# x of the batches 1 to 7 rounded by a casting transfer, its remainders by an accumulating transfer

## The chip, the cores and the metric

The kernel runs on one core of a Trainium2 chip. The metric is the device time of one execution in microseconds (us); the lower, the better. The kernel before takes 455.5 us in the median of three runs (455.4 to 455.71).

## The reference

The input x has 8 batches of 256 tokens with 1024 features, in float32. Two layers follow one another.

```python
x = x + ffn0(quantize(x))          # quantize: 8 levels of thresholds, each with its step and zero point
x = x + ffn1(cond1(x))
# ffn0: router logits x @ router_w.T over 4 experts, softmax over the best 2, low-rank deltas A (16 x 1024), B
# cond1: x @ W.T + 0.5 * (x @ lora_A[label of the batch]) @ lora_B_w.T
# ffn1: x @ kernel + bias + two low-rank products (one gated for each batch, one shared)
```

Everything that is linear in x is folded into one matrix P of 1024 x 1024, so that the output of a batch is x @ P plus a bias and low-rank terms. The low-rank terms of the first layer depend on the quantised x.

## The kernel before, in words

P is made first, in 16 steps (8 row tiles for each of 2 halves of the columns), each on TensorE from W and the kernel matrix. Each operand of these products is held as a rounded part (`hi`, of a type to which the value is rounded) and the remainder (`lo`), and a product is three matmuls: hi x hi, hi x lo, lo x hi.

Then comes the loop over 8 batches with 8 slots each, 64 slots q in all. The output of a batch has 4 tiles (2 blocks of tokens, 2 halves of the columns), and two slots make one tile: a matmul of the bias (L1088) opens it, then 12 matmuls a slot (4 of the 8 feature tiles k, three products each: L1090 x_hi by p_hi, L1091 x_hi by p_lo, L1092 x_lo by p_hi), and `close` (L1067) adds the low-rank terms from zt and tb. zt of a batch holds three things: u-projections of x, made by `z_begin` from xs, the unrounded x (L994, L998, in slot 4 of the batch before); the turned gated middle (`gated_turn` L980, copied by ACT in L493); and, when `z_end` (L1005) has closed the former, ACT's copy of it (L635). Only after that copy may TensorE run the `close` of the batch.

The quantisation of batches runs ahead of the products, in 64 groups (8 batches x 8 levels), laid over the slots by the table `GROUPS`. A group is, on ACT, `levels` (L426) and `raise_levels` (L439), on DVE a TENSOR_SCALAR (L662), the mask (L671, a TENSOR_SCALAR) and the merge (L680, COPY_PREDICATED). The first group of a batch also has ACT's magnitude (L416). `mid` (L970) on TensorE then projects the quantised batch. The engines' programs are written out by hand: each runs its own list in its own order and waits on semaphores.

The places that the change touches:
- POOL's queue holds only `quant_input`: the loads of x into xq, for the quantisation, of the batches 1 to 7 (L303). The load for batch c waits until all the levels of batch c - 2 are made.
- SP's queue loads x into xs (L383 for batch 0, `xs_load` L385 to L390 for the others), the adapters and rows, and stores the output (L399, L404).
- `x_part` on ACT (L495 to L502) rounds xs into x_hi, in two parts of 128 x 1024 elements for a batch; `x_part` on DVE (L789 to L793) subtracts x_hi from xs into x_lo. For batch 0 both come right before the loop; for batch b + 1 they come in batch b, on ACT in the slots 1 and 3 (`XAT` in L238, called at L648), on DVE one slot later (L874).
- x_hi and x_lo have two places each, used in turn; `x_done` says that a batch's matmuls have read theirs (L1094).
- TensorE waits for x_lo at the first slot of each batch (L1074).
- Ahead of the loop, after the last P step, DVE also makes the bias (L864), ACT bu (L509).

Of the kernel before, what the change touches and what calls it, by code (L numbers as in the profile page):

```python
# [26 lines left out]
F32 = mybir.dt.float32  # L27
# [4 lines left out]
ALU = mybir.AluOpType  # L32
ACT = mybir.ActivationFunctionType
# [3 lines left out]
BATCH = 8  # L37
# [15 lines left out]
STEPS = HALVES * KT  # L53
# [10 lines left out]
def build(nc, a, out_t, itok):  # L64
# [98 lines left out]
    sem = nc.alloc_semaphore  # L163
# [34 lines left out]
    mg_made, mgt_full, mgt_made = sem("mg_made"), sem("mgt_full"), sem("mgt_made")  # L198
    x_hi_made, x_lo_made = sem("x_hi_made"), sem("x_lo_made")
    bet_hi_made, bet_lo_made, bpfull, bp_made = sem("bet_hi_made"), sem("bet_lo_made"), sem("bpfull"), sem("bp_made")  # L200
# [36 lines left out]

    XAT, ZAT = (1, 3), 4  # L238

# [52 lines left out]
    with nc.allow_non_contiguous_dma(reason="rows of 1 KB and small constants"), nc.Block() as block:  # L292

        @block.gpsimd
        def _(pool):

            def quant_input(c):
                if c == 1:
                    pool.wait_ge(w_in[0], 16 * 2)
                if c >= 2:  # L300
                    pool.wait_ge(levels_made, (c - 1) * G)
                    pool.wait_ge(abs_made, c - 1)
                pool.dma_start(xq[:, c % 2], x_v[c]).then_inc(xq_in[c % 2], 16)  # L303

            for c in range(1, BATCH):
                quant_input(c)

        @block.sync
        def _(sp):
# [75 lines left out]
            def xs_load(b):  # L385
                sp.wait_ge(x_lo_made, b * XPARTS)
                sp.wait_ge(z_read, b)
                sp.dma_start(xs, x_v[b]).then_inc(xs_in, 16)
                if b + 1 < BATCH:
                    adapters(b + 1)  # L390
# [21 lines left out]
        def _(act):  # L412
# [81 lines left out]

            def x_part(c, p):  # L495
                act.wait_ge(xs_in, 16 * (c + 1))
                if c < 2:
                    act.wait_ge(ofull, STEPS)
                else:
                    act.wait_ge(x_done, c - 1)  # L500
                part = slice(p * XK, (p + 1) * XK)
                nc.scalar.activation(x_hi[:, c % 2, part], xs[:, part], ACT.Copy).then_inc(x_hi_made, 1)  # L502

# [118 lines left out]
            for p in range(XPARTS):  # L622
                x_part(0, p)
            for c, g in GROUPS[STEPS + 1]:
# [3 lines left out]
            for q in range(BATCH * KT + LAG + 1):  # L628
# [19 lines left out]
                if b + 1 < BATCH and j in XAT:  # L648
                    x_part(b + 1, XAT.index(j))
                if b + 1 < BATCH and j == ZAT:  # L650
# [6 lines left out]
        def _(dve):  # L657
# [130 lines left out]

            def x_part(c, p):  # L789
                dve.wait_ge(x_hi_made, c * XPARTS + p + 1)  # L790
                part = slice(p * XK, (p + 1) * XK)
                nc.vector.tensor_tensor(x_lo[:, c % 2, part], xs[:, part], x_hi[:, c % 2, part].bitcast(F32),
                                        ALU.subtract).then_inc(x_lo_made, 1)  # L793
# [67 lines left out]
            for p in range(XPARTS):  # L861
                x_part(0, p)
            dve.wait_ge(bias_hi_made, 1)
            nc.vector.tensor_tensor(bias[R:2 * R], bias_raw[R:2 * R], bias[R:2 * R].bitcast(F32),  # L864
                                    ALU.subtract).then_inc(bias_made, 1)
            for b in range(BATCH):
                for j in range(KT):
                    ranks(slot(b, j))
                    for c, g in GROUPS[slot(b, j)]:
                        quant(c, g)  # L870
                    if b == 0 and j == 0:
                        for h in range(HALVES):
                            bp_add(h)
                    if b + 1 < BATCH and j - 1 in XAT:  # L874
                        x_part(b + 1, XAT.index(j - 1))

        @block.tensor
        def _(pe):
# [191 lines left out]
            for q in range(BATCH * KT):  # L1070
                b, j = divmod(q, KT)
                n, part = divmod(q, 2)
                s, (t, h) = b % 2, divmod(n % TILES, HALVES)
                if j == 0:  # L1074
                    pe.wait_ge(x_lo_made, (b + 1) * XPARTS)
                if part == 0:
# [77 lines left out]
```

## Time and profile before

| | us |
|---|---|
| median of 3 runs | 455.5 |
| the profiled execution's own time | 455.03 |
| its span, first to last instruction | 453.2 |
| TensorE (PE) busy | 445.7, 98% |
| DVE busy | 392.8, 87% |
| ACT busy | 357.7, 79% |
| POOL busy | 7.9, 2% |
| DMA from POOL's queue (q0) | 7.34 MB, 4.8% of the 16 engines' span |
| DMA from SP's queue (q1) | 42.66 MB, 29.6% |

PE is TensorE's matmul, PEld its weight load; DVE is VectorE, ACT ScalarE, POOL GpSimd, SP SyncE. Busy times of PE are modelled from pipelined matmuls, so a busy PE does not mean PE at its peak. L502 is line 502 of the kernel. A wait is the idle time of an engine ahead of an instruction, with what released it. The granted clock of TensorE is at full speed over the whole run (1.000).

### The profile page before, as it was taken

To read this page: it belongs to the slowest core of one execution; us is meant where nothing else is said; L and a number is where in the kernel's file an instruction comes from. 1 tells how busy PE (TensorE), PEld (TensorE's weight loads), DVE (VectorE), ACT (ScalarE), POOL (GpSimd) and SP (SyncE) were. 2 spreads that over 40 slices of the span, in tenths; PEclk is the share of its full clock that TensorE was granted. 3 is DMA by queue.
4 is the path that set the end of the run, shared out by engine and by line. 5 is a ranking of instruction groups with operands and counts; after the bars stand their busy time and mean duration, and the time that the engine had idled before them with its cause. 6 is when DMAs were issued, how large, how long until landed. Compare 5 with 4: busy or idle time off the path is not lost.

```text
span 453.2 us, 5629 instructions
## 1 busy us (share of the span) xinstructions
PE 445.7 (98%) x2166; PEld 348.3 (77%) x2166; DVE 392.8 (87%) x392; ACT 357.7 (79%) x296; POOL 7.9 (2%) x11
## 2 busy tenths in 40 slices
PE   8979999999999999999999999999999999999997
PEld 8847778888878887778767877777778777867883
DVE  1696979999999999999999999999987999899410
ACT  1579999946989969898997899959697899778002
POOL 0000000000000000100000000000200000000000
PEclk9999999999999999999999999999999999999999
DMA  7999535200562153214125107105414003101102
GB/s 271 358 311 410 140 82 175 58 1 0 167 204 92 53 135 100 78 39 156 59 93 162 59 25 232 58 2 162 152 31 132 29 29 140 58 1 46 48 1 93
DMA packets 36124, 50.35 MB, mean 111 GB/s; under 512 B 26658, under 2 KB 26914, under 8 KB 33826
## 3 DMA queue, kind: packets, MB, share of 16 engines
q1 hardware_dynamic: 35090, 42.66, 29.6%
q0 software_dynamic: 1008, 7.34, 4.8%
q8 instruction: 17, 0.28, 0.3%
q14 instruction: 9, 0.07, 0.1%
HBM read 39.51 MB, written 10.49 MB: 110 GB/s over the span
## 4 chain that ended last, share of the span: by engine, by line
PE 92%; SPq 4%; DMA 3%; issue 1%; ACT 0%
PE bank L1090 13%; PE bank L1092 13%; PE bank L1091 13%; PE bank L970 6%; PE bank L1067 6%; PE bank L1027 6%; PE bank L1032 6%; PE bank L1028 6%; PE bank L998 6%; PE bank L939 5%; DMA lb<-lb_in 3%; PE bank L1088 2%; PE bank L994 2%; PE bank L1005 1%; PE bank L958 1%; SPq L327 1%
## 5 line engine op out<-in xcount | busy, mean ns | idle before, releaser
L680 DVE COPY_PREDICATED val<-inside,val 128x2048 f32<-128x2048 uint8 x56 | 143.3, 2559 | 0.3
L439 ACT ACTIVATE val<-level,shift,small 128x2048 f32<-128x2048 int16 x64 | 133.9, 2093 | 3.7 <-PE bank L970 3.7
L426 ACT ACTIVATE level<-xq,inv 128x2048 int16<-128x2048 f32 x64 | 127.7, 1997 | 0.6
L1090 PE MATMUL bank<-p_hi,x_hi 128*128 128x512 f32 x256 | 102.8, 402 | 0.0
L1092 PE MATMUL bank<-p_hi,x_lo 128*128 128x512 f32 x256 | 100.1, 391 | 0.0
L1091 PE MATMUL bank<-p_lo,x_hi 128*128 128x512 f32 x256 | 100.0, 391 | 0.0
L662 DVE TENSOR_SCALAR val<-val,width,unshift 128x2048 f32<-128x2048 f32 x64 | 87.2, 1363 | 3.1 <-ACT val L439 3.0
L671 DVE TENSOR_SCALAR inside<-absx,thr 128x2048 uint8<-128x2048 f32 x56 | 72.7, 1299 | 0.0
L1090 PEld LDWEIGHTS bank<-p_hi,x_hi 128*128 128x128 f32 x256 | 48.1, 188 | 17.1 <-issue 8.5
L1091 PEld LDWEIGHTS bank<-p_lo,x_hi 128*128 128x128 f32 x256 | 48.1, 188 | 10.5 <-issue 0.7
L1092 PEld LDWEIGHTS bank<-p_hi,x_lo 128*128 128x128 f32 x256 | 48.1, 188 | 10.5
L1027 PE MATMUL bank<-kp_hi,w_hi 128*128 128x512 f32 x128 | 51.1, 399 | 2.1 <-DVE kp_lo L728 2.1
L1032 PE MATMUL bank<-kp_hi,w_lo 128*128 128x512 f32 x128 | 50.4, 394 | 0.0
L1028 PE MATMUL bank<-kp_lo,w_hi 128*128 128x512 f32 x128 | 49.9, 390 | 0.0
L1067 PE MATMUL bank<-tb,zt 128*128 128x512 f32 x64 | 32.1, 595 | 0.0
L970 PEld LDWEIGHTS bank<-ra,val 128*128 128x128 f32 x256 | 29.8, 192 | 1.8 <-issue 1.4
L1027 PEld LDWEIGHTS bank<-kp_hi,w_hi 128*128 128x128 f32 x128 | 24.1, 188 | 7.1 <-issue 2.5
L970 PE MATMUL bank<-ra,val 128*128 128x68 f32 x256 | 29.5, 273 | 0.0
L998 PE MATMUL bank<-xs,ub 128*64 128x256 f32 x128 | 29.3, 382 | 0.0
L939 PE MATMUL bank<-aefft,wst 128*128 128x256 f32 x128 | 29.2, 380 | 0.0
L1032 PEld LDWEIGHTS bank<-kp_hi,w_lo 128*128 128x128 f32 x128 | 24.1, 188 | 5.3
L1028 PEld LDWEIGHTS bank<-kp_lo,w_hi 128*128 128x128 f32 x128 | 24.1, 188 | 4.7
(98 smaller groups left out, 447.0 us busy)
## 6 DMA issues: line engine op xcount, KB each, us to landing
xs<-xt_in SPq DMA_DIRECT2D x8, 1024.0 KB, 4.9
wst<-w_in SPq DMA_DIRECT2D x14, 512.0 KB, 5.0
xq<-xt_in POOLq DMA_DIRECT2D x7, 1024.0 KB, 6.6
out_t<-ost SPq DMA_DIRECT2D x14, 512.0 KB, 4.0
la<-la_in SPq DMA_DIRECT2D x4, 512.0 KB, 5.4
kst<-k_in SPq DMA_DIRECT2D x4, 512.0 KB, 13.7
lb<-lb_in SPq DMA_DIRECT2D x4, 512.0 KB, 14.4
kst<-k_in SPq DMA_DIRECT2D x1, 2048.0 KB, 10.8
```

Of the source, the lines that this page charges most:

```text
L426: nc.scalar.activation(level[:, g % 2], xq[:, c % 2], ACT.Copy, scale=inv[:, group(g)]).then_inc(levels_made, 1)
L439: nc.scalar.activation(val[:, turn(c, g)], level[:, g % 2], ACT.Relu, bias=shift[:, group(g)], scale=par[:, 1, group(g)]).then_inc(raised, 1)
L662: nc.vector.tensor_scalar(v, v, width[:, group(g)], unshift[:, group(g)], ALU.min, ALU.add).then_inc(valued, 1)
L671: nc.vector.tensor_scalar(inside[:, g % 2], absx, thr[:, group(g)], None, ALU.is_gt).then_inc(masked, 1)
L680: nc.vector.copy_predicated(val[:, acc(c)], inside[:, g % 2], val[:, turn(c, g)]).then_inc(merged, 1)
L970: last = mm(midbank[:, t * RT:(t + 1) * RT], val[:, acc(c), k, t * P:(t + 1) * P], ra[:, k], start=k == 0, stop=k == KT - 1)
L1027: mm(obank[n % RING], w_hi[side(n)][:, o], kp_hi[:, o], start=o == 0, stop=False)
L1028: mm(obank[n % RING], w_hi[side(n)][:, o], kp_lo[:, o], start=False, stop=False)
L1032: last = mm(obank[n % RING], w_lo[side(n)][:, o], kp_hi[:, o], start=False, stop=o == KT - 1)
L1090: mm(o, x_hi[:, s, k, at], p_hi[:, h, k], start=False, stop=False)
L1091: mm(o, x_hi[:, s, k, at], p_lo[:, h, k], start=False, stop=False)
L1092: last = mm(o, x_lo[:, s, k, at], p_hi[:, h, k], start=False, stop=False)
```

## The change

Batch 0 stays as it was. For the batches 1 to 7, POOL issues a transfer of x from memory into x_hi that casts to the rounded type. ACT writes the negative of x_hi into x_lo, in two parts, now in the slots 2 and 4 of the batch before. POOL issues for each part a transfer of x that adds to what stands in x_lo, so that x_lo becomes x minus x_hi. DVE's subtraction goes for these batches. POOL's queue has a new order: the loads of xq for the batches 1 to 3, then for each batch c its `x_split` and after it the load of xq for batch c + 3. TensorE waits at the start of a batch for x_hi and for both additions, and the load of xs by SP waits only for batch 0's x_lo and for the reading of xs by TensorE.

```diff
--- before.py
+++ after.py
@@ -196,7 +196,8 @@
     mid_made, gate_step, gap_made, exp_made = sem("mid_made"), sem("gate_step"), sem("gap_made"), sem("exp_made")
     gates_made = sem("gates_made")
     mg_made, mgt_full, mgt_made = sem("mg_made"), sem("mgt_full"), sem("mgt_made")
-    x_hi_made, x_lo_made = sem("x_hi_made"), sem("x_lo_made")
+    x_hi_made, x_lo_made, x_hi_in, x_neg_made, x_lo_in = (
+        sem(n) for n in ("x_hi_made", "x_lo_made", "x_hi_in", "x_neg_made", "x_lo_in"))
     bet_hi_made, bet_lo_made, bpfull, bp_made = sem("bet_hi_made"), sem("bet_lo_made"), sem("bpfull"), sem("bp_made")
     bp_lo_made, bp_copied = sem("bp_lo_made"), sem("bp_copied")
     mg_zeroed = sem("mg_zeroed")
@@ -235,7 +236,7 @@
     OUT_AT = OUT
     OUT = {at: c for c, at in OUT_AT.items()}
 
-    XAT, ZAT = (1, 3), 4
+    XAT, ZAT = (2, 4), 4
 
 
     V_AT = (4, 10)
@@ -302,8 +303,23 @@
                     pool.wait_ge(abs_made, c - 1)
                 pool.dma_start(xq[:, c % 2], x_v[c]).then_inc(xq_in[c % 2], 16)
 
+            def x_split(c):
+                if c == 1:
+                    pool.wait_ge(ofull, STEPS)
+                else:
+                    pool.wait_ge(x_done, c - 1)
+                pool.dma_start(x_hi[:, c % 2], x_v[c]).then_inc(x_hi_in, 16)
+                for p in range(XPARTS):
+                    part = slice(p * XK, (p + 1) * XK)
+                    pool.wait_ge(x_neg_made, (c - 1) * XPARTS + p + 1)
+                    pool.dma_start(x_lo[:, c % 2, part], x_v[c][:, part], accum_op=ALU.add).then_inc(x_lo_in, 16)
+
+            for c in range(1, 4):
+                quant_input(c)
             for c in range(1, BATCH):
-                quant_input(c)
+                x_split(c)
+                if c + 3 < BATCH:
+                    quant_input(c + 3)
 
         @block.sync
         def _(sp):
@@ -383,7 +399,7 @@
             sp.dma_start(xs, x_v[0]).then_inc(xs_in, 16)
 
             def xs_load(b):
-                sp.wait_ge(x_lo_made, b * XPARTS)
+                sp.wait_ge(x_lo_made, XPARTS)
                 sp.wait_ge(z_read, b)
                 sp.dma_start(xs, x_v[b]).then_inc(xs_in, 16)
                 if b + 1 < BATCH:
@@ -492,14 +508,17 @@
                     act.wait_ge(ofull, STEPS + (c - ZSLOTS + 1) * TILES)
                 nc.scalar.activation(zt[2 * R:P, c % ZSLOTS], mgbank[ER:2 * ER, 0:TOK], ACT.Copy).then_inc(mgt_made, 1)
 
-            def x_part(c, p):
-                act.wait_ge(xs_in, 16 * (c + 1))
-                if c < 2:
-                    act.wait_ge(ofull, STEPS)
-                else:
-                    act.wait_ge(x_done, c - 1)
+            def x_part(p):
+                act.wait_ge(xs_in, 16)
+                act.wait_ge(ofull, STEPS)
                 part = slice(p * XK, (p + 1) * XK)
-                nc.scalar.activation(x_hi[:, c % 2, part], xs[:, part], ACT.Copy).then_inc(x_hi_made, 1)
+                nc.scalar.activation(x_hi[:, 0, part], xs[:, part], ACT.Copy).then_inc(x_hi_made, 1)
+
+            def x_neg(c, p):
+
+                act.wait_ge(x_hi_in, 16 * c)
+                part = slice(p * XK, (p + 1) * XK)
+                nc.scalar.activation(x_lo[:, c % 2, part], x_hi[:, c % 2, part].bitcast(F32), ACT.Copy, scale=-1.0).then_inc(x_neg_made, 1)
 
             def bu_out(c):
 
@@ -620,7 +639,7 @@
             p_out(STEPS - 1)
 
             for p in range(XPARTS):
-                x_part(0, p)
+                x_part(p)
             for c, g in GROUPS[STEPS + 1]:
                 quant(c, g)
             bp_lo_out()
@@ -646,7 +665,7 @@
                 if slot(b, j) in EXP:
                     gate_exp(EXP[slot(b, j)])
                 if b + 1 < BATCH and j in XAT:
-                    x_part(b + 1, XAT.index(j))
+                    x_neg(b + 1, XAT.index(j))
                 if b + 1 < BATCH and j == ZAT:
                     bu_out(b + 1)
             for n in range(BATCH * TILES):
@@ -786,10 +805,10 @@
                 nc.vector.tensor_tensor(mg[:, :, ER:2 * ER].rearrange("p t (e r) -> p t e r", e=E), mid[:, :, 0:ER].rearrange("p t (e r) -> p t e r", e=E),
                                         gates.unsqueeze(3).to_broadcast([P, TT, E, R0]), ALU.mult).then_inc(mg_made, 1)
 
-            def x_part(c, p):
-                dve.wait_ge(x_hi_made, c * XPARTS + p + 1)
+            def x_part(p):
+                dve.wait_ge(x_hi_made, p + 1)
                 part = slice(p * XK, (p + 1) * XK)
-                nc.vector.tensor_tensor(x_lo[:, c % 2, part], xs[:, part], x_hi[:, c % 2, part].bitcast(F32),
+                nc.vector.tensor_tensor(x_lo[:, 0, part], xs[:, part], x_hi[:, 0, part].bitcast(F32),
                                         ALU.subtract).then_inc(x_lo_made, 1)
 
             for m in range(KT // 4, KT // 2):
@@ -859,7 +878,7 @@
                 ranks(n)
             p_out(STEPS - 1)
             for p in range(XPARTS):
-                x_part(0, p)
+                x_part(p)
             dve.wait_ge(bias_hi_made, 1)
             nc.vector.tensor_tensor(bias[R:2 * R], bias_raw[R:2 * R], bias[R:2 * R].bitcast(F32),
                                     ALU.subtract).then_inc(bias_made, 1)
@@ -871,8 +890,6 @@
                     if b == 0 and j == 0:
                         for h in range(HALVES):
                             bp_add(h)
-                    if b + 1 < BATCH and j - 1 in XAT:
-                        x_part(b + 1, XAT.index(j - 1))
 
         @block.tensor
         def _(pe):
@@ -1071,8 +1088,11 @@
                 b, j = divmod(q, KT)
                 n, part = divmod(q, 2)
                 s, (t, h) = b % 2, divmod(n % TILES, HALVES)
-                if j == 0:
-                    pe.wait_ge(x_lo_made, (b + 1) * XPARTS)
+                if q == 0:
+                    pe.wait_ge(x_lo_made, XPARTS)
+                elif j == 0:
+                    pe.wait_ge(x_hi_in, 16 * b)
+                    pe.wait_ge(x_lo_in, 16 * b * XPARTS)
                 if part == 0:
                     if n < RING:
                         pe.wait_ge(ofree, STEPS)
```

## Rows read from the trace of the kernel before

**Rows 1.** busy time of TensorE, and the chain that ended last (page)
```profile
PE 445.7 (98%) x2166; PEld 348.3 (77%) x2166; DVE 392.8 (87%) x392; ACT 357.7 (79%) x296; POOL 7.9 (2%) x11
...
PE 92%; SPq 4%; DMA 3%; issue 1%; ACT 0%
```

**Rows 2.** TensorE's waits: for what, us in total, times, longest
```profile
PE bank L1027 <- DVE kp_lo L728: 2.1, 1, 2.1
```

**Rows 3.** groups of lines: busy us, mean ns | idle before
```profile
L792 DVE TENSOR_TENSOR x_lo<-xs,x_hi 128x1024 fp32r<-128x1024 f32 x16 | 19.9, 1249 | 0.7 <-ACT x_hi L502 0.7
...
L502 ACT ACTIVATE x_hi<-xs 128x1024 fp32r<-128x1024 f32 x16 | 16.7, 1047 | 0.4 <-DMA xs<-xt_in 0.3
```

**Rows 4.** landing of the loads of L303: all seven, then the one at 317.8
```profile
DMA to landing us min/median/max: 5.1/6.6/9.1
...
DMA to landing us min/median/max: 8.0/8.0/8.0
```

**Rows 5.** stretches: busy time of each engine, clock, DMA share, GB/s
```profile
192.00:193.00 1.00, 1.00 (x6) 0.80 (x5) 1.00 (x2) 1.00 (x1) 0.00 (x0) 1.00 1.00 426
...
166.00:167.00 1.00, 1.00 (x6) 0.81 (x6) 1.00 (x2) 0.00 (x0) 0.00 (x0) 1.00 1.01 131
...
320.00:327.00 7.00, 7.00 (x33) 5.30 (x32) 7.00 (x5) 3.02 (x5) 0.17 (x1) 1.00 0.79 246
```

**Rows 6.** ACT's timeline: start us, us, line, operation, idle before
```profile
199.91 0.22 ACT L509 ACTIVATE bu<-bank 64x64 f32<-64x64 f32 x1
...
287.85 0.58 ACT L532 ACTIVATE ost<-bank 128x512 f32<-128x512 f32 x1
...
315.48 2.01 ACT L426 ACTIVATE level<-xq,inv 128x2048 int16<-128x2048 f32 x1
...
321.72 0.38 ACT L493 ACTIVATE zt<-bank 64x256 f32<-64x256 f32 x1 [0.81 <-PE bank L980]
325.27 0.38 ACT L635 ACTIVATE zt<-bank 64x256 f32<-64x256 f32 x1 [3.16 <-PE bank L1005]
```

**Rows 7.** TensorE's timeline
```profile
213.12 0.48 PE L1088 MATMUL bank<-bias,ones 128*128 128x512 f32 x1
...
278.88 1.02 PE L1067 MATMUL bank<-tb,zt 128*128 128x512 f32 x2
...
314.97 0.80 PE L1088 MATMUL bank<-bias,ones 128*128 128x512 f32 x1
...
328.04 1.88 PE L1067 MATMUL bank<-tb,zt 128*128 128x512 f32 x4
...
343.86 3.68 PE L970 MATMUL bank<-ra,val 128*128 128x68 f32 x32
```

**Rows 8.** POOL's timeline
```profile
229.12 0.53 POOL L303 DMA_DIRECT2D xq<-xt_in  x1 [39.54 <-ACT level L426]
...
317.78 2.39 POOL L303 DMA_DIRECT2D xq<-xt_in  x1 [43.83 <-ACT level L426]
```

**Rows 9.** DVE's timeline, end of P and around 318 us
```profile
164.75 1.27 DVE L671 TENSOR_SCALAR inside<-absx,thr 128x2048 uint8<-128x2048 f32 x1
...
317.51 1.34 DVE L662 TENSOR_SCALAR val<-val,width,unshift 128x2048 f32<-128x2048 f32 x1
...
319.96 2.54 DVE L680 COPY_PREDICATED val<-inside,val 128x2048 f32<-128x2048 uint8 x1
```

**Rows 10.** timelines of ACT, DVE and TensorE at the loop's start
```profile
169.92 2.01 ACT L502 ACTIVATE x_hi<-xs 128x1024 fp32r<-128x1024 f32 x2 [0.30 <-DMA xs<-xt_in]
...
181.08 0.37 ACT L493 ACTIVATE zt<-bank 64x256 f32<-64x256 f32 x1
...
173.40 1.22 DVE L864 TENSOR_TENSOR bias<-bias_raw,bias 32x1024 fp32r<-32x1024 f32 x1
...
176.63 0.50 PE L1088 MATMUL bank<-bias,ones 128*128 128x512 f32 x1
...
183.00 0.64 PE L1005 MATMUL bank<-zt,bu 64*64 64x256 f32 x2
```

## The prediction, made before the changed kernel ran

> **What bounds the kernel now.** I read the page first. TensorE is busy for 445.7 of 453.2 us and the chain that ended last is 92% TensorE [rows 1]. Busy matmul time is modelled, so the next view is the list of TensorE's waits: four entries in the whole run, the longest 2.1 us on DVE's kp_lo [rows 2], and asked of 170 to 453 us alone the list is empty. So in the batch loop TensorE waits for nothing, and relief of another engine has nothing there to give back. The change can only make new waits. The working therefore asks, for every edit, at what time its result is wanted and at what time it will be there.
>
> **The change, part by part.** *DVE:* 14 of the 16 subtractions at L792 go, 1249 ns each, 17.5 us [rows 3]. No TensorE wait of the loop ends at DVE, so they are worth nothing; their cover is TensorE's own work. *ACT:* 14 copies at L502 become 14 negations of the same shape, 1047 ns each [rows 3]; I price them the same. They move one or two slots later (slots 2 and 4 of a batch, where they stood in 1 and 3). They now wait for the casting transfer (x_hi), and behind a waiting negation stand, on ACT, the quantisation of the next groups, the evictions (L532) and the zt copy (L635) that TensorE's closing matmuls (L1067) need. *SP:* its loads of xs no longer wait for x_lo, so they come no later than before: nothing. *POOL:* its queue gets 7 casting and 14 accumulating transfers between the loads of xq.
>
> *Casting and accumulating transfers.* The trace has neither. The nearest row is a plain 1 MB load from POOL, 5.1, 6.6 and 9.1 us from issue to landing (minimum, median, maximum) [rows 4]; in the middle it moves 426 GB/s [rows 5], 2.5 us for 1.05 MB. I bound a cast by that below and by twice the movement above (an estimate: 5 us of movement), and take it near the plain one, because size and rows are the same. An accumulation of 512 KB reads two sides, so I bound it by half a plain load below and by 9.1 us above.
>
> *Are the accumulations in time?* The tightest is batch 1. Its second negation stands in slot 4, after the quantisation and ahead of the L509 that ran at 199.91; it ends at about 201.0 [rows 6]. Batch 1 begins with the L1088 at 213.12 [rows 7]. That is 12.1 us for issue and landing, against at most 9.1. In the later batches more work of TensorE lies between slot 4 and the next start, and the same count gives more. Cost: 0.
>
> *Is x_hi in time for the first negation?* It is issued when the batch before last is done and wanted in slot 2 of the next. Tightest where nothing else interferes is batch 4: issue 278.9 at the close of batch 2, ACT free after L635 and L532 at about 287.4 (287.85 + 0.58 less the 1.04 of the L502 that has left) [rows 6, 7]. That is 8.5 us against a median of 6.6: at most a short wait of ACT, and what TensorE wants of ACT next, zt and the eviction, stands ahead of the negation in slot 2. Cost: 0.
>
> *Batch 5 is another matter.* The new order on POOL is xq(7), then x_hi(5), and xq(7) still waits for the last level of batch 5. That level is the L426 which began at 315.48; POOL's L303 followed at 317.78 [rows 6, 8]. TensorE freed the slot for x_hi(5) with batch 3, just ahead of the L1088 at 314.97 [rows 7], so the order costs 3 us at once. And the issue of xq(7) itself held POOL for 2.39 us, where that of 229.12 took 0.53 [rows 8]. In those 2.39 us DVE ran two TENSOR_SCALARs, the first from 317.51, and POOL was free just after COPY_PREDICATED began at 319.96 [rows 9]. The Trainium skill, SBUF — State Buffer, section on who interferes with whom, says that DVE in a mode with both ports locks GpSimd out of the shared pair, so that it cannot write descriptors; the trace agrees (2.39 against 0.53 us). DVE and ACT have the same work between 307 and 318 us as before, so I let the 2.39 us stand; without that lock all of the following comes 1.9 us earlier.
>
> So xq(7) lands at 317.78 + 8.0 = 325.8 [rows 4]. x_hi(5) is behind it in the same queue, with the store of the output beside both. Another 1.05 MB takes 2.5 us at 426 GB/s and 4.3 us at the mean of 320 to 327 us, 246 GB/s [rows 5]; I take 2.9, nearer the former because the queue is full by then. Landing: 328.7. ACT is free for the negation at 322.1, after L493 (321.72 + 0.38) [rows 6], and waits 6.6 us. Then negation 1.05, zt copy 0.38, about 0.1 for handing over: zt stands at 330.2. TensorE wants it for the L1067 at 328.04, whose weights are loaded some 0.2 us earlier [rows 7]. Before, zt was there at 325.65, 2.2 us early. **New wait: 330.2 - 327.8 = 2.4 us**, bounds 2.0 and 3.8 with the two rates, 0.5 without the lock. Behind it ACT is some 5 us late. Its last value for batch 5 (L439) then ends near 334 and DVE's merge some 4 us later, 338; the L970 that wants it begins at 343.86 [rows 7]. The second negation of batch 5 ends near 341, and batch 5 begins a whole L970 product and three slots after 343.86. No further wait.
>
> *The start of the loop.* x_hi(1) is now issued with the first load of xs, both at the end of the last P step, so they share the DMA engines. DVE's TENSOR_SCALAR of 164.75 keeps POOL from its descriptors until about 166 [rows 9], so x_hi(1) moves from about 167. By then 0.13 of the 1.05 MB of xs had moved (131 GB/s over 166 to 167, engines full [rows 5]); the other 0.92 MB were in when ACT began on them at 169.92, 2.9 us later [rows 10]. At half of 426 GB/s they take 4.3 us, and with some 0.5 for completion 4.8: xs comes about 2.0 us late. On ACT everything from the L502 at 169.92 to the L493 at 181.08 follows directly; on DVE the bias at 173.40 [rows 10]. The bias is then ready at 176.6, as TensorE wants it (176.63). zt is ready at 181.45 + 2.0 = 183.45, and TensorE wants it ahead of 183.00, at 182.8 [rows 10]. **New wait: 0.6 us**; bounds 0 (xs late by under 1.3 us) and 1.9 (a cast that holds the engines twice as long: xs 3.3 us late).
>
> **Sum.** 0 for DVE, 0 for ACT's own work, +0.6 at the start, +2.4 at the close of batch 4: +3.0 us. The profiled execution has 455.03 us (span 453.2 and 1.8 around it), 0.5 under the median of 455.5. On the median the forecast is 458.5 us.
>
> **Rivals.**
> 1. *Nothing is late.* The POOL queue is not held at 317.78: xq(7) is issued in 0.5 us, x_hi(5) moves at the full 426 GB/s and lands by 326.3, from which point zt is ready by 327.8 and TensorE never waits; and xs is late by less than 1.3 us. Then 455.5. For it: two of the three conditions lie within 2.5 us of the rows, and DVE is relieved. Against: ACT, not DVE, times the level that POOL waits for, and ACT's row there does not change. Chance 0.21.
> 2. *The new transfers are much slower than plain ones.* A cast at half the rate lands x_hi(5) 2.9 us later, wait 5.3, and the first wait is 1.9: +7.2, 462.7. Slower still, ACT waits in every batch; an accumulation over 12 us adds its excess to each of seven batch starts, so 14 us would give 7 x 2 more, some 473. For it: no row shows either kind of transfer. Against: size and partitions are those of the plain load. Chance 0.22.
> 3. *DVE's relief shows.* If lateness of DVE delayed TensorE unseen, 17.5 us less of it could give up to about 1 us: 454.5. Against: no wait on DVE in the loop. Chance 0.03.
> 4. *The forecast*, two short waits: 0.54, between 457 and 460.5.
>
> **How the numbers follow.** Rival 1 with rival 3 is the lower part; rival 2 begins at 460.5 and most of it ends by 464. Range 455.4 to 464. A measurement of this kernel tells 0.2%, 0.9 us, from no change. Faster than 454.6: 0.03. Within: 0.20, nearly all of rival 1. Slower than 456.4: the forecast, rival 2 and what is left of rival 1, 0.77.
>
> **What would show it.** In the new profile: the list of TensorE's waits has one entry at the closing matmul (L1067, its weight load) near 328 us, released by ACT's zt copy, of 2 to 4 us, and one of under 2 us near 183 us. ACT has its longest wait of the loop at the negation of batch 5, 6 to 7 us, on the casting transfer. POOL's issue of x_hi(5) follows directly on that of xq(7), at 318 to 320 us. DVE's busy time falls by 17.5 us to some 375. The accumulations land in less than 9 us and no batch start waits for x_lo. I am wrong if TensorE waits at batch starts (rival 2), if ACT waits for x_hi in several batches, or if POOL passes xq(7) before 315 us (rival 1).

## The result: 461.7 us against 455.6, some 1.0% slower

Over four executions of each kernel, the changed kernel has a median of 461.69 us (458.44 to 463.1) and the kernel before 455.61 us (455.4 to 457.17). The ratio is 1.0105, 95% interval 1.0073 to 1.0137. The forecast was 458.5 us, the range 455.4 to 464: the loss is about twice the 3.0 us that were forecast, and still inside the range.

The profiled execution of the changed kernel took 460.35 us, 5.3 us more than that of before (455.03). In this section the lines of code are those of the changed kernel: L304 the load of xq, L311 the casting transfer, L315 the accumulating one, L521 the negation, L509 and L654 the two zt copies of a batch, L1084 its closing matmuls.

The page, where [rows 1] and [rows 3] stood: busy time, DMA queue of POOL, chain, and the groups of the operations that the change touches.

```profile
span 458.6 us, 5622 instructions
...
PE 448.4 (98%) x2166; PEld 349.7 (76%) x2166; DVE 377.9 (82%) x378; ACT 357.4 (78%) x296; POOL 31.6 (7%) x32
...
q0 software_dynamic: 4032, 22.02, 18.4%
...
PE 86%; DMA 5%; SPq 4%; ACT 3%; issue 1%; POOL 1%; ACTq 0%
...
L681 DVE TENSOR_SCALAR val<-val,width,unshift 128x2048 f32<-128x2048 f32 x64 | 86.5, 1352 | 19.9 <-ACT val L455 19.6
...
L315 POOL DMA_DIRECT2D x_lo<-xt_in x14 | 20.4, 1461 | 148.3 <-ACT x_lo L521 148.3
```

DVE has 14.9 us less work. It spends what it gained in waiting for ACT's val: 19.6 us of idle time ahead of L681. TensorE's busy time, which should not change at all, is 2.7 us longer: that is a clock, as shown below. The chain has 3% of ACT and 1% of POOL in it, where it had 0% and none.

TensorE's waits (columns as in [rows 2]):

```profile
PE bank L1084 <- ACT zt L654: 3.4, 1, 3.4
PE bank L1044 <- DVE kp_lo L747: 2.1, 1, 2.1
```

One wait is new, and it is the only one of the batch loop. The three timelines around it, POOL's first ([rows 8]):

```profile
317.78 2.38 POOL L304 DMA_DIRECT2D xq<-xt_in  x1 [17.92 <-ACT level L442]
320.15 0.56 POOL L311 DMA_DIRECT2D x_hi<-xt_in  x1
```

ACT's ([rows 6]):

```profile
321.71 0.38 ACT L509 ACTIVATE zt<-bank 64x256 f32<-64x256 f32 x1 [1.76 <-PE bank L997]
330.03 1.06 ACT L521 ACTIVATE x_lo<-x_hi 128x1024 fp32r<-128x1024 f32 x1 [7.94 <-DMA x_hi<-xt_in]
331.11 0.38 ACT L654 ACTIVATE zt<-bank 64x256 f32<-64x256 f32 x1
```

TensorE's ([rows 7]):

```profile
327.79 0.39 PE L1112 MATMUL bank<-p_hi,x_lo 128*128 128x512 f32 x1
331.55 2.77 PE L1084 MATMUL bank<-tb,zt 128*128 128x512 f32 x4 [3.37 <-ACT zt L654]
333.33 1.41 PE L1108 MATMUL bank<-bias,ones 128*128 128x512 f32 x1
```

Read from left to right: POOL issues x_hi(5) only at 320.15, behind xq(7), whose issue held it for 2.38 us. ACT is done with L509 at 322.1, and its next instruction is the negation. It waits there for 7.94 us, with the zt copy behind it, which needs nothing of x_hi(5). So L1084 starts at 331.55, where its counterpart of before started at 328.04.

The four L1084 together took 2.77 us, those of before 1.88 [rows 7]. The stretches say why (columns as in [rows 5]; the clock is the first figure behind POOL's count):

```profile
332.00:333.00 1.00, 1.00 (x3) 0.43 (x2) 0.00 (x0) 1.00 (x1) 0.52 (x1) 0.80 0.07 16
333.00:334.00 1.00, 1.00 (x3) 0.33 (x1) 0.00 (x0) 1.00 (x2) 0.00 (x0) 0.50 0.46 53
334.00:335.00 1.00, 1.00 (x4) 0.69 (x3) 0.00 (x0) 1.00 (x1) 0.00 (x0) 0.50 0.96 188
335.00:336.00 1.00, 1.00 (x4) 0.81 (x3) 0.60 (x1) 0.97 (x2) 0.00 (x0) 0.50 0.97 193
336.00:337.00 1.00, 1.00 (x6) 0.82 (x5) 0.97 (x2) 1.00 (x1) 0.00 (x0) 0.99 0.47 90
```

After its idle 3.4 us TensorE's granted clock is 0.50 of 2.4 GHz, the lower level of 1.2 GHz, for some 3.4 us (0.4 + 3 + 0.02, the shortfall of each slice doubled). Work of that length at half speed costs half of it, 1.7 us. The other readings of the change's price: 331.55 - 328.04 = 3.5 us, and 3.5 + 1.7 = 5.2 of the 5.4 us by which the span grew (458.6 against 453.2).

There is a second stretch of this kind in this profile, behind the 2.1 us wait at L1044:

```profile
20.00:30.00 10.00, 7.94 (x29) 6.18 (x28) 9.94 (x19) 8.95 (x12) 0.00 (x0) 0.83 1.04 310
```

It costs next to nothing where it lies here, from 25.4 to 28.8 us: TensorE has to wait for its input at some 32 us anyway, and L975 starts at 32.77, as its counterpart of before did at 32.80 without any half clock. The number of such stretches serves below as a count. Each takes 0.004 off the mean clock of an execution (1.7 us lost of 458). So 0.996 is one of them, 0.992 or 0.993 two. Every execution has its mean clock on record, and only the profiled ones a trace. The mean clock counts the stretches; it does not say where they lie, and that matters below.

### The profile page after: what moved, and what is told of

Its sections match the earlier page's. It is cut to its first block, busy times and chain, and to the rows that moved or that the text cites. A ratio compares the mean times of both kernels' runs of the same rounds, so it can differ in the third digit from the quotient of the medians.

```text
span 458.6 us, 5622 instructions
## 1 busy us (share of the span) xinstructions
PE 448.4 (98%) x2166; PEld 349.7 (76%) x2166; DVE 377.9 (82%) x378; ACT 357.4 (78%) x296; POOL 31.6 (7%) x32
## 4 chain that ended last, share of the span: by engine, by line
PE 86%; DMA 5%; SPq 4%; ACT 3%; issue 1%; POOL 1%; ACTq 0%
PE bank L1110 12%; PE bank L1112 11%; PE bank L1111 11%; PE bank L987 6%; PE bank L1044 6%; PE bank L1049 6%; PE bank L1045 6%; PE bank L1084 6%; PE bank L956 5%; PE bank L1015 5%; DMA lb<-lb_in 3%; DMA x_hi<-xt_in 2%; PE bank L1011 2%; PE bank L1108 2%; ACT level L442 2%; ACT val L455 1%
## 5 line engine op out<-in xcount | busy, mean ns | idle before, releaser
L681 DVE TENSOR_SCALAR val<-val,width,unshift 128x2048 f32<-128x2048 f32 x64 | 86.5, 1352 | 19.9 <-ACT val L455 19.6
L1110 PEld LDWEIGHTS bank<-p_hi,x_hi 128*128 128x128 f32 x256 | 48.4, 189 | 17.5 <-issue 8.8
L1044 PE MATMUL bank<-kp_hi,w_hi 128*128 128x512 f32 x128 | 51.7, 404 | 2.1 <-DVE kp_lo L747 2.1
L1084 PE MATMUL bank<-tb,zt 128*128 128x512 f32 x64 | 33.0, 610 | 3.4 <-ACT zt L654 3.4
L315 POOL DMA_DIRECT2D x_lo<-xt_in x14 | 20.4, 1461 | 148.3 <-ACT x_lo L521 148.3
L1044 PEld LDWEIGHTS bank<-kp_hi,w_hi 128*128 128x128 f32 x128 | 24.5, 191 | 7.3 <-issue 2.5
(101 smaller groups left out, 456.6 us busy)
```

Of the source, the lines that this page charges most:

```text
L681: nc.vector.tensor_scalar(v, v, width[:, group(g)], unshift[:, group(g)], ALU.min, ALU.add).then_inc(valued, 1)
L1044: mm(obank[n % RING], w_hi[side(n)][:, o], kp_hi[:, o], start=o == 0, stop=False)
L1110: mm(o, x_hi[:, s, k, at], p_hi[:, h, k], start=False, stop=False)
```

## Experiments

The first sets ask which part of the change makes the wait; the later ones ask what the wait costs. Ratios are to the kernel before on the same chip.

**The order on POOL alone.** The casting transfer of batch 5 is issued ahead of xq(7); everything else is as changed.

```
...
-                x_split(c)
+                if c != 5:
+                    x_split(c)
+                x_add(c)
+                if c == 4:
+                    x_split(5)
```

> Only POOL's order is changed: the cast of x for batch 5 is issued ahead of the load of xq for batch 7. My theory (the cast of batch 5 stands behind that load, ACT waits for it, and TensorE waits for the zt copy behind ACT): the cast is issued at about 315 us and lands by 321, ACT waits under 0.5 us at the negation of batch 5, TensorE has no wait in the loop, the granted clock is 1.00 after 300 us and the time is 455.5 us, ratio to before 0.999 to 1.001. Rival (the 14 MB more that move cost time everywhere, or the cast and the additions do): the time stays above 457 us.

Measured: 455.69 us (454.73 to 460.46, 12 executions), ratio 0.9988 [0.9965, 1.0011]. POOL's timeline, then ACT's:

```profile
314.64 0.55 POOL L311 DMA_DIRECT2D x_hi<-xt_in  x1 [16.34 <-PE bank L1118]
317.45 2.30 POOL L304 DMA_DIRECT2D xq<-xt_in  x1 [2.25 <-ACT level L448]
```

```profile
321.80 1.06 ACT L527 ACTIVATE x_lo<-x_hi 128x1024 fp32r<-128x1024 f32 x1
324.94 0.38 ACT L660 ACTIVATE zt<-bank 64x256 f32<-64x256 f32 x1 [2.08 <-PE bank L1028]
```

The transfer leaves three us earlier, the negation starts on time, and the whole loss is gone, with all 7 casts and all 14 accumulations still there. So none of these costs anything that this measurement can tell (the interval reaches 0.23% to either side), and the place of one transfer in one queue costs the 1%. It is no gain either: the interval holds 1. The slowest of the twelve executions, 460.46 us, has a mean clock of 0.993, that is a second half clock, in a kernel whose profile has no wait in the loop.

**The order on ACT alone.** POOL's queue stays as changed; the first negation of batch 5 moves one slot on, behind the zt copy.

```
+                at = (3, 4) if b == 4 else XAT
-                if b + 1 < BATCH and j in XAT:
-                    x_neg(b + 1, XAT.index(j))
+                if b + 1 < BATCH and j in at:
+                    x_neg(b + 1, at.index(j))
```

> POOL's order stays as in the changed kernel; only the first negation of batch 5 moves on ACT from slot 2 to slot 3, behind the zt copy that the closing matmuls of batch 4 need. My theory (it is the place on ACT that carries the lateness to TensorE, not the lateness of the transfer): the cast still lands at about 330 us, ACT's wait for it is under 1 us, TensorE waits nowhere in the loop and the time is 455.5 us. Rival (TensorE would also be stopped by what else is late, the levels or x_lo of batch 5): a TensorE wait at the matmuls of the quantised batch 5 or at the start of batch 5, above 456.5 us.

Measured: 456.93 us (454.87 to 457.57, 10), ratio 0.9995 [0.9977, 1.0012]. x_hi(5) is as late as in the changed kernel (issued at 322.23 behind a 2.38 us issue of xq(7), in a program that is some 2 us later from its start on: its first batch starts at 178.70 us, that of the changed kernel at 176.61), and TensorE waits for nothing in the loop. ACT's timeline:

```profile
327.34 0.38 ACT L654 ACTIVATE zt<-bank 64x256 f32<-64x256 f32 x1 [3.16 <-PE bank L1023]
...
332.20 1.07 ACT L521 ACTIVATE x_lo<-x_hi 128x1024 fp32r<-128x1024 f32 x1 [0.60 <-DMA x_hi<-xt_in]
```

So it is not the late transfer that costs either, but that zt stands behind the negation in ACT's order. Either link taken out frees TensorE.

**Each kind of transfer alone.** With the casts only, DVE still subtracts (in the slots 2 and 4, as before) and POOL issues a cast once DVE is done with x_lo of the batch ahead. With the accumulations only, ACT still rounds from xs and then negates.

```
-                for p in range(XPARTS):
-                    part = slice(p * XK, (p + 1) * XK)
-                    pool.wait_ge(x_neg_made, (c - 1) * XPARTS + p + 1)
-                    pool.dma_start(x_lo[:, c % 2, part], x_v[c][:, part], accum_op=ALU.add).then_inc(x_lo_in, 16)
...
+                    if b + 1 < BATCH and j in XAT:
+                        x_part(b + 1, XAT.index(j))
```

> Half of the change: x_hi of the batches 1 to 7 comes from the casting transfer, in the changed kernel's order on POOL (the load of xq for batch 7 ahead of the cast of batch 5), but x_lo is DVE's subtraction again and there is neither negation nor addition. The cast of batch 5 should still land at about 330 us; now DVE waits for it, behind the merge of a group, and ACT does not, so zt of batch 4 is there at 325.7 us. My theory: no TensorE wait in the loop, 455.5 us, ratio 0.998 to 1.002, although the cast is just as late. Rival (a late cast costs wherever it is waited for): DVE's lateness reaches the matmuls of the quantised batch 5 near 344 us, above 457 us.

```
-                pool.dma_start(x_hi[:, c % 2], x_v[c]).then_inc(x_hi_in, 16)
...
+                if b + 1 < BATCH and j in (1, 3):
+                    x_part(b + 1, (1, 3).index(j))
```

> The other half: x_hi is ACT's copy of xs again, in slots 1 and 3, and x_lo is ACT's negation in slots 2 and 4 plus the accumulating transfer, so ACT has 14 instructions of 1.05 us more than in either kernel (14.7 us) and no instruction of it waits for a transfer from POOL. My theory: additions land in 5 to 9 us, well before the batches begin, ACT has the room, no TensorE wait, 455.5 to 456.2 us. Rival (the additions or the fuller ACT cost): TensorE waits at batch starts or at closing matmuls, above 457 us.

Measured: casts only 456.43 us (454.33 to 458.56, 10), ratio 1.0004 [0.9983, 1.0025]; accumulations only 456.05 us (455.12 to 457.1, 10), ratio 0.9993 [0.9976, 1.0011]. Neither list of TensorE's waits has an entry in the loop. With casts only, the late x_hi(5) is there too, but it is DVE that waits for it, and that wait reaches no instruction of TensorE:

```profile
329.61 1.23 DVE L810 TENSOR_TENSOR x_lo<-xs,x_hi 128x1024 fp32r<-128x1024 f32 x1 [2.99 <-DMA x_hi<-xt_in]
```

The loss needs both halves of the change: the cast that is late, and the negation on ACT that waits for it.

**The lock.** DVE holds its TENSOR_SCALAR of 317.5 back until xq(7) has been issued; a one-element memset on POOL tells it.

```
...
+                if c == 4:
+                    nc.gpsimd.memset(flag, 0.0).then_inc(issued, 1)
...
+                if (c, g) == (5, 5):
+                    dve.wait_ge(issued, 1)
```

> The changed kernel with its order, but DVE holds back the value of group 5 of batch 5 (its TENSOR_SCALAR at 317.5 us) until POOL has issued the load of xq for batch 7. If DVE's TENSOR_SCALARs kept POOL from issuing: that issue takes about 0.5 instead of 2.4 us, the cast of batch 5 is issued at 318.9 and lands at about 328.2 instead of 330, and TensorE's wait for zt falls from 3.5 to about 1.6 us; ratio to before some 1.004, plus what the clock takes. If the 2.4 us have another cause: issue and wait stay at 2.4 and 3.5 us.

Measured: 457.29 us (456.12 to 459.37, 12), ratio 1.0028 [1.0011, 1.0046]. POOL's timeline, DVE's, and TensorE's:

```profile
318.19 0.55 POOL L305 DMA_DIRECT2D xq<-xt_in  x1 [17.91 <-ACT level L445]
318.73 0.12 POOL L325 MEMSET flag<- 128x1 f32 x1
318.77 1.58 POOL L312 DMA_DIRECT2D x_hi<-xt_in  x1
```

```profile
318.88 1.35 DVE L684 TENSOR_SCALAR val<-val,width,unshift 128x2048 f32<-128x2048 f32 x1 [0.86 <-POOL flag L325]
```

```profile
329.64 1.98 PE L1089 MATMUL bank<-tb,zt 128*128 128x512 f32 x4 [1.05 <-ACT zt L657]
```

The issue of xq(7) takes 0.55 us where it took 2.38: the long issue was DVE's doing. Now the held TENSOR_SCALAR runs into the next issue and stretches that to 1.58 us. xq(7) lands 5.3 us after its issue (8.4 in the changed kernel), x_hi(5) 9.3 us after its own (9.9), and the wait is 1.05 us instead of 3.4. So the lock on xq(7)'s issue makes 2.3 of the 3.4 us; the order, with the shorter lock that is left, makes 1.

**The wait filled with matmuls.** 14 matmuls on an unused bank stand ahead of the wait for zt, so that TensorE works through most of it while zt comes as late as in the changed kernel.

```
...
+                    if c == 4:
+                        pe.wait_ge(taken, 13)
+                        for _ in range(FILL):
+                            mm(cols[18 % CRING], ones, bias[:, 0:HALF], start=True, stop=True)
```

> The changed kernel, but TensorE runs 14 more matmuls of 512 columns (about 3.2 us at 0.23 us each) ahead of its wait for zt of batch 4; their result is overwritten. The wait for zt ends when it did, about 331.5 us, since ACT sets it. Theory of the clock (the 1.8 us beyond the wait came from a clock that fell because TensorE had stood idle): no half clock after 331 us, span 453.2 + 3.5 = 456.7 and time 458.5 us. Rival (the clock falls for another reason, such as the transfers or the time since start): half clock again at 332 to 336 us, time above 460 us as in the changed kernel.

> The changed kernel once more, to see what differs between its executions, which lay between 458.4 and 463.1 us. If the wait at the close of batch 4 and the clock after it are all: TensorE's wait is 3 to 4 us in every profile and only the length of the stretch at half clock varies, total 458.5 to 461. If something else is late in the slower executions, such as the cast of another batch: this profile may show a second TensorE wait or a second stretch at half clock.

> The changed kernel with 14 matmuls ahead of TensorE's wait for zt of batch 4, for more executions. Six of eight executions of the changed kernel showed a mean granted clock of 0.992 or 0.993, that is two stretches at the half clock, and the other two 0.995; before never showed less than 0.996 in 23. Theory (the second stretch follows from TensorE standing idle for 3.5 us): with the idle time filled, 0.993 or less in at most one of four executions, and a median 1.5 to 2.5 us under the changed kernel's. Rival (the second stretch has to do with the transfers): 0.993 in most executions and the changed kernel's median.

Against the same executions of the kernel before, the filled kernel had 460.28 us (458.78 to 462.93, 4), ratio 1.0099 [1.0064, 1.0135], and the changed kernel once more 462.25 us (458.4 to 463.34, 4), ratio 1.0131 [1.01, 1.0162]. The intervals overlap, so that pair settled nothing. The repeat with more executions gave the filled kernel 458.89 us (458.1 to 460.69, 7), ratio 1.0058 [1.0036, 1.0079], clear of the changed kernel's 1.0131 and touching the lower end of its first 1.0105 [1.0073, 1.0137]. (These ratios are to the kernel before in different sets; only the first pair shares one, and it alone would not carry the reading.) Its TensorE:

```profile
327.82 3.41 PE L1123 MATMUL bank<-bias,ones 128*128 128x512 f32 x14
...
331.11 1.99 PE L1085 MATMUL bank<-tb,zt 128*128 128x512 f32 x4
```

L1085 starts no earlier than L1084 of the changed kernel less the 0.4 us by which x_hi(5) came sooner here, so the delay by zt is the same, and yet about half of the loss is gone (0.58% against 1.05 and 1.31%). What differs is the clock: of the 11 filled executions 10 have 0.995 to 1.0 and one 0.993. Of the 8 of the changed kernel 6 have 0.992 or 0.993 and two 0.995, and these two are its fastest, 458.40 and 458.44 us. One of them is the profiled one of the repeat, and its trace shows a wait of 3.5 us with no half clock behind it, span 456.6 = 453.2 + 3.5 (less 0.1):

```profile
330.00:335.00 5.00, 3.77 (x13) 2.48 (x14) 0.00 (x0) 4.98 (x4) 0.91 (x1) 1.00 0.45 65
```

**The wait without the transfers.** The kernel before, unchanged but for 15, 11 or 8 chained copies of 0.66 us on ACT into a scratch tile, ahead of the zt copy of batch 4.

```
...
+                if q == 34:
+                    act.wait_ge(ra_in, 16)
+                    for i in range(15):
+                        if i:
+                            act.wait_ge(filled, i)
+                        nc.scalar.activation(ust.rearrange("p a b -> p (a b)"), ra.rearrange("p k r -> p (k r)")[:, 0:2 * BATCH * R], ACT.Copy).then_inc(filled, 1)
```

> The kernel before, with none of the new transfers: ACT makes 15 chained copies of 0.6 us (an estimate) into a scratch tile ahead of the zt copy of batch 4, so that zt is ready near 331.5 us as in the changed kernel, and TensorE's wait at the closing matmul is about 3.4 us. Theory (the cost is TensorE's idle of 3.4 us and the half clock behind it, not anything the transfers do besides): ratio 1.008 to 1.014, and a mean clock of 0.992 to 0.993 in most executions. Rival (the transfers cost beside the wait, or the clock falls because of them): ratio about 1.007 or less, the mean clock at 0.995 to 0.996 as before.

> The same with 11 copies: zt near 329 us, a wait of TensorE of about 1 us, as in the kernel without the lock. Theory: ratio 1.001 to 1.003 and no execution at 0.993. Rival (any idle there costs the clock): ratio over 1.005 and a mean clock of 0.992 to 0.993.

> Eight copies, some 5.3 us of ACT at 0.66 us each: zt near 327.1 us, just in time, with ACT as late behind it as in the changed kernel's loop. Theory (only TensorE's wait and what the clock does behind it cost): no wait or one under 0.4 us at the closing matmul, ratio 0.999 to 1.002, mean clock as in the kernel before. Rival (ACT's lateness itself costs later in the loop): ratio 1.005 or more without a wait at the closing matmul.

> Eleven copies once more, for a second profile and median. If the first median (4 us above the kernel before with a wait of 1.7 us in its profile) was a matter of that set of executions, the ratio is now 1.003 to 1.006; if eleven copies cost more than the wait seen, it is again 1.008 to 1.011, and this profile should show where: a wait or a half clock beside those of the first profile.

| copies | TensorE's wait for zt, us | median us (n) | ratio | executions by mean clock |
|---|---|---|---|---|
| 8 | none | 455.81 (12) | 1.0004 [0.9982, 1.0026] | 12 at 0.995 to 1.0 |
| 11 | 1.7 | 459.45 (6) | 1.0093 [1.0062, 1.0123] | 5 at 0.996 to 1.0, 1 at 0.993 |
| 11, again | 1.7 | 458.93 (6) | 1.0064 [1.0043, 1.0085] | 6 at 0.995 to 0.996 |
| 15 | 4.3 | 464.19 (6) | 1.0193 [1.0164, 1.0221] | 2 at 0.992 to 0.993, 4 at 0.989 |

Eight copies hold ACT up for 5.3 us and cost nothing measurable: lateness of ACT is free as long as zt is in time. Fifteen copies give TensorE a wait of 4.3 us, with no transfer added anywhere, and the same picture as the changed kernel (waits, then ten-microsecond stretches):

```profile
PE bank L1073 <- ACT zt L635: 4.3, 1, 4.3
```

```profile
330.00:340.00 10.00, 7.77 (x35) 5.00 (x36) 3.88 (x3) 9.91 (x9) 0.00 (x0) 0.83 0.01 2
```

DMA is idle there (2 GB/s), and the clock falls all the same. So the half clock needs no transfer: it comes behind TensorE's idle, though not every time, as the profile with 3.5 us of wait and none shows. The profiled execution adds up, 453.2 + 4.3 + 1.7 = 459.2. My numbers for this run (up to 1.014) were too low: the wait came out 0.9 us longer than I meant it to be, and four of six executions have a third stretch at half clock that the profiled one lacks. Where it lies I can't say, and with 1.7 us it would not be all of the 3.2 us by which the median lies above the profiled execution, which is the fastest of the six.

Eleven copies cost 3 to 4 us by the medians where the wait is 1.7. I had expected 1.001 to 1.003 and no execution at 0.993, and was wrong in both; the repeat, 1.0064, falls between the two answers that I had set it. The second profile shows part of the answer. Both have the same wait at L1073, and the spans are 454.6 and 457.0: the second program is 2.5 us late by 40 us already (329.66 against 327.19 at the last matmul ahead of the wait, TensorE busy without a break from 40 us on in both), with this wait in its first 40 us, which the first doesn't have, and a mean clock of 0.96 there:

```profile
PE bank L951 <- DMA alt<-alt_in: 1.8, 1, 1.8
```

In this profile the half clock lies elsewhere than in the changed kernel's: from 33.3 to 36.7 us, behind that wait, and not from 25.4 to 28.8. L964, the first matmul behind the input, starts at 33.38 where the first program has 32.29, and its four matmuls take 2.04 us instead of 1.15. So a mean clock of 0.996 stands for two cases. Six kept profiles have an early stretch. With the stretch at 25 to 30 us (both of the changed kernel, the one with DVE held and the one with 15 copies) the first batch starts at 176.2 to 177.0 us, as before (176.63); with the stretch at 33 to 38 us (this one, and likewise the kernel with accumulations only) it starts at 178.5 and 178.7. It is not the only cause of a late start: the kernel with zt ahead of the negation starts at 178.70 with a clock of 1.000.

Such a start is not special to that kernel: in all sets some executions of the kernel before take 457 to 459 us too. But eleven executions of twelve had more than the wait alone explains. A single half clock behind the wait of 1.7 us, with none at the start, would also read 0.996 and give 453.2 + 1.7 + 1.7 = 456.6, as an estimate from these rows; neither profile shows that case. Why there are so many stays open.

## Why the prediction was right, and where it was off

**DVE's relief, 0.** Right. 14.9 us less (377.9 against 392.8), not 17.5: instructions on DVE follow each other somewhat sooner than each lasts (1.12 us from a subtraction to the next start, for 1.23 of duration), so the mean of a group times its count is more than the busy time. That is some 1.5 of the 2.6 us between the two; the rest was not traced. It was worth nothing that shows, and DVE now waits for ACT.

**Casts and accumulations priced by the plain load.** Right. The casts of 1 MB landed in 5.0 to 9.9 us, median 5.5, the plain loads from POOL had 6.6 before [rows 4] and, behind other transfers now, 8.4; so rival 2's slow cast falls. The accumulations of 512 KB landed in 5.4 to 8.6 us, median 6.4, under the bound of 9.1, and no batch start waited for them.

**Batch 5.** The mechanism was as forecast, link by link: xq(7) ahead of x_hi(5), the issue held 2.4 us (2.38), ACT at the negation with zt behind it, TensorE at the closing matmul. The Trainium skill's rule on who interferes with whom (SBUF — State Buffer) agrees with the run in which DVE was held: 0.55 us instead of 2.38. The size was off. I had 2.4 us of wait, between 2.0 and 3.8; it was 3.4. The step that was mis-sized is the 2.9 us from xq(7)'s landing to that of x_hi(5): it took 3.85 us (326.2 to 330.05, from the issue at 320.15 and the 9.9 us of that transfer). Another 0.4 us comes from xq(7) itself, which landed 8.4 us after its issue, not 8.0. What made the step longer is the movement: the rate of 426 GB/s did not hold to the end, and part of it was not for x_hi(5):

```profile
326.00:327.00 1.00, 1.00 (x6) 0.82 (x5) 1.00 (x1) 0.00 (x0) 0.00 (x0) 1.00 1.11 430
327.00:328.00 1.00, 1.00 (x6) 0.63 (x4) 0.24 (x1) 0.00 (x0) 0.00 (x0) 1.00 1.66 315
328.00:329.00 1.00, 0.18 (x1) 0.00 (x0) 0.00 (x0) 0.00 (x0) 0.00 (x0) 1.00 1.37 344
329.00:330.00 1.00, 0.00 (x0) 0.00 (x0) 0.00 (x0) 0.00 (x0) 0.00 (x0) 1.00 0.06 8
```

From 326 to 329 us 1.09 MB moved (430 + 315 + 344); by queue 0.91 MB of it were POOL's, that is x_hi(5), and 0.18 MB SP's, mostly the store of the output. So x_hi(5) had some 300 GB/s, and its movement ended at about 329.0. ACT could start at 330.03, 1.0 us later. I had put in nothing for that, as I took both landings to have it behind them; that holds in part, since xq(7)'s last bytes moved at about 325.6, some 0.6 us ahead of its landing. So of the step's extra 0.95 us about 0.4 is the longer tail and the rest the shared movement. The mean rate of 246 GB/s, my upper end, would have given 4.3 us. Without the lock I had 0.5 us; it was 1.05, as the lock moved to the next issue.

**The start of the loop, +0.6.** Wrong: 0. I let the xs load and x_hi(1), issued at the same moment, share the DMA engines half and half. They didn't. ACT began on xs at 169.93, as before (169.92 [rows 10]), and TensorE wants nothing that isn't there:

```profile
169.93 2.01 ACT L515 ACTIVATE x_hi<-xs 128x1024 fp32r<-128x1024 f32 x2 [0.44 <-DMA xs<-xt_in]
```

The traffic around it:

```profile
166.00:167.00 1.00, 1.00 (x6) 0.81 (x6) 1.00 (x1) 0.00 (x0) 0.04 (x1) 1.00 0.66 147
167.00:168.00 1.00, 1.00 (x6) 0.84 (x5) 1.00 (x1) 0.00 (x0) 0.00 (x0) 1.00 0.98 410
168.00:169.00 1.00, 1.00 (x7) 0.81 (x5) 0.96 (x8) 0.20 (x2) 0.00 (x0) 1.00 0.99 418
```

From 166 to 169 us 0.98 MB moved. By queue it was 119 packets (0.96 MB) of SP's, that is xs, and 2 packets (0.02 MB) of POOL's, x_hi(1). The one issued first (165.11 against 165.38) was served first. The Trainium skill, DMA: Bandwidth & Descriptors, section on queues, rings and completion order, says that each DMA engine goes round the queues for which it has work, but drains a whole packet, typically of some 9 to 17 descriptors, before it switches. Each of the two transfers is 144 entries in the profile, 9 on each of the 16 DMA engines; if these are the descriptors that the Trainium skill counts, a whole transfer fits into one of its packets, and its rule would give what was measured and not the half and half that I took. Whether SP's queue goes first as such or only because its issue was earlier, no run tells.

**What the sum lacked.** The clock. After the wait TensorE ran at half speed for some 3.4 us, which added 1.7 us to the profiled execution and shows in six of eight mean clocks. The profile of before has no such stretch (mean clock 1.000), so none of its rows priced it, and I priced a new idle of TensorE by its own length alone, with no bound for the clock behind it. By terms: forecast 0.6 + 2.4 = 3.0; measured 0 + 3.5 + 1.7 = 5.2 in the profile. The two omissions that pull up are larger than the one that pulls down, so the median lies above the 457 to 460.5 that I gave for the forecast's own case. It lies inside the whole range, though only because that was drawn wide for a cause (slow transfers) that did not occur. In that the prediction was lucky: the chain of waits was forecast, and the size that makes the median fit was not.

**What is left of the difference.** The median of the changed kernel is 1.3 us above its profiled execution, and two of its four executions take 463.0. These two count as many half clocks as the profiled one (0.992 and 0.993 against 0.993), so the rest is no third stretch. It could be the place of the first: with it at 33 to 37 us, as in the second run with 11 copies, the program is some 2.5 us late, against 2.7 here. No profile of the changed kernel shows it, and it is not settled.

**The rivals.** 1, nothing late: out, the interval of the ratio is above 1. It is what the kernel would do with the order on POOL or on ACT changed: 455.69 and 456.93 us. 2, slow transfers: its time is right and its reason wrong, as the batches other than 5 show no wait of ACT for x_hi at all. 3, relief that shows: no version came out faster than the kernel before beyond its interval. In rival 2 the sum was off as well: 14 us more on top of its own 462.7 are 476.7, and the 473 of the text is the forecast of 458.5 with the same 14.

## What to carry to other kernels

Here TensorE waited for nothing in the loop, and moving 14.9 us of work from DVE to DMA gave nothing back. In such a kernel the place to look is the order of the queues: which transfer now stands behind which, and what urgent instruction stands behind the one that waits. A new wait should be put after the urgent instruction, or its transfer ahead of the one that is bound by something later; here either alone took the whole loss away. And a wait of TensorE has to be priced with the clock behind it, which here was half as much again in the profile, and by the mean clocks in six executions of eight.

## What the runs showed that I had not expected

- An issue on POOL for an accumulating transfer took 0.86 to 2.27 us (median 1.59), for a cast 0.54 to 1.06 (median 0.60). The difference goes with what DVE does at the time, as most accumulations are issued into TENSOR_SCALARs; it was not separated.
- A wait of TensorE of 3.4 or 3.5 us was followed by a half clock of some 3.4 us in one profile and by none in another of the same kernel. By the mean clocks the first is the more frequent, 6 of 8. Behind a wait of 1.0 to 1.7 us one execution in 24 has a second stretch; with the 3.4 us filled by matmuls, one in 11. But one in 54 has it too in the variants whose profiles have no wait in the loop, so a single case says little about the wait ahead of it.
- Freeing an engine from one lock put the same lock on its next issue (1.58 us): DVE and POOL shared the time anew, rather than each being quicker.
